# Four steps to a partition: rows of x and of the output in pieces of 4 KB, and the output product reading rwkv at every fourth step

## The reference

```python
xx = jnp.pad(x, ((0, 0), (1, 0), (0, 0)))[:, :-1]
xk = x * time_mix_k + xx * (1.0 - time_mix_k)        # xv, xr likewise
k = jnp.einsum('btc,dc->btd', xk, Wk)                # v, and sr = sigmoid(...), likewise
w = -jnp.exp(time_decay)
rwkv = sr * _wkv(w, time_first, k, v)                # a recurrence over the steps
attn = jnp.einsum('btc,dc->btd', rwkv, Wo)
x = _layernorm(x + attn, axis=-1)
gate = x @ wg.T; up = x @ wu.T                       # weights are int32 values times 1/127
x = _layernorm(x + (silu(gate) * up) @ wd.T, axis=-1)
```

## Time and profile before

| | us |
|---|---|
| median of 3 runs | 290.96 |
| lowest, highest | 290.49, 291.65 |
| the profiled execution | 292.65 |
| its span, from first to last instruction | 290.8 |

### The profile page before, as it was taken

The page is one execution under the profiler, slowest core; times in us unless marked ns, Lnnn a source line. Parts: engine busy times, 40 slices in busy tenths (PEclk is TensorE's granted clock), DMA queues, the critical chain, the costliest instruction groups (busy, mean ns, idle before and its releaser), DMA issues.

```text
span 290.8 us, 4281 instructions
## 1 busy us (share of the span) xinstructions
PE 274.8 (95%) x1258; PEld 199.7 (69%) x1258; DVE 260.5 (90%) x451; ACT 215.1 (74%) x388; POOL 192.0 (66%) x155
## 2 busy tenths in 40 slices
PE   7999988889999999999999999999999999999990
PEld 5745555646695689657885679558974789778890
DVE  4995599899999998999999999999899999889763
ACT  3486798389667988689966986698858882799472
POOL 3637699979968875986868775986566580334043
PEclk9999999999999999999999999999999999999996
DMA  7900600220102202030204011210201020102003
GB/s 239 371 4 0 220 1 0 72 72 3 36 0 76 72 1 72 18 129 0 72 5 133 11 37 35 72 36 0 72 22 51 1 74 0 36 2 73 0 3 113
DMA packets 13541, 16.26 MB, mean 56 GB/s; under 512 B 720, under 2 KB 11216, under 8 KB 13520
## 3 DMA queue, kind: packets, MB, share of 16 engines
q1 hardware_dynamic: 12832, 15.48, 16.3%
q10 hardware_dynamic: 688, 0.53, 0.6%
HBM read 11.81 MB, written 4.19 MB: 55 GB/s over the span
## 4 chain that ended last, share of the span: by engine, by line
PE 74%; DVE 12%; ACT 9%; issue 2%; DMA 1%; SPq 0%; DVEq 0%; ACTq 0%
PE bank_b L1153 12%; PE bank_a L1153 12%; PE bank_a L1176 11%; PE bank_b L1109 9%; PE bank_a L1072 7%; PE bank_d L1072 7%; PE bank_c L1072 7%; PE bank_b L1130 2%; DMA wkT<-wk 1%; DVE rwkv L786 1%; DVE state L746 1%; ACT L605 1%; PE bank_d L1099 1%; ACT wts L491 1%; PE bank_d L1088 1%
## 5 line engine op out<-in xcount | busy, mean ns | idle before, releaser
L403 POOL TENSOR_TENSOR hlo<-hid,hhi 128x512 fp32r<-128x512 f32 (+1 forms) x36 | 53.3, 1484 | 31.6 <-ACT hhi L583 31.5
L376 POOL TENSOR_SCALAR wts<-gap,par 128x512 f32<-128x512 f32 (+1 forms) x18 | 35.9, 1994 | 25.4 <-DVE gap L714 24.6
L499 ACT ACTIVATE mix<-dx,par 128x512 f32<-128x512 f32 x48 | 31.4, 712 | 19.0 <-POOL dx L356 19.0
L1176 PE MATMUL bank_a<-wd_r,hhi 128*128 128x256 f32 x180 | 44.2, 287 | 1.0 <-POOL hlo L403 0.9
L1176 PE MATMUL bank_a<-wd_r,hlo 128*128 128x256 f32 x180 | 42.8, 279 | 0.0
L362 POOL TENSOR_TENSOR mix<-mix,xt 128x512 f32<-128x512 f32 (+1 forms) x36 | 40.7, 1163 | 0.3 <-ACT mix L499 0.3
L1176 PEld LDWEIGHTS bank_a<-wd_r,hhi 128*128 128x128 f32 x180 | 33.8, 188 | 3.5 <-issue 2.6
L583 ACT ACTIVATE hhi<-hid 128x512 fp32r<-128x512 f32 (+1 forms) x54 | 31.0, 576 | 4.7 <-DVE hid L862 4.7
L491 ACT ACTIVATE wts<-wts 128x512 f32<-128x512 f32 (+1 forms) x54 | 27.9, 577 | 8.4 <-DVE wts L723 8.2
L862 DVE TENSOR_TENSOR hid<-bank_b,act 128x512 f32<-128x512 f32 (+1 forms) x48 | 30.8, 643 | 3.6 <-issue 1.1
L1176 PEld LDWEIGHTS bank_a<-wd_r,hlo 128*128 128x128 f32 x180 | 33.8, 188 | 0.3 <-issue 0.2
(11 more groups left out here) (127 smaller groups left out, 600.0 us busy)
## 6 DMA issues: line engine op xcount, KB each, us to landing
xrow<-x SPq DMA_DIRECT2D x7, 512.0 KB, 3.8
xt<-xT SPq DMA_DIRECT2D x6, 513.0 KB, 3.6
out<-y_buf SPq DMA_DIRECT2D x6, 512.0 KB, 2.9
wg_i<-wg SPq DMA_DIRECT2D x1, 768.0 KB, 8.4
wu_i<-wu SPq DMA_DIRECT2D x1, 768.0 KB, 9.8
wd_i<-wd SPq DMA_DIRECT2D x1, 768.0 KB, 11.5
out<-y_buf SPq DMA_DIRECT2D x3, 256.0 KB, 2.2
xt<-xT SPq DMA_DIRECT2D x2, 257.0 KB, 2.9
```

Source lines behind the costliest of these rows:

```text
L376: nc.gpsimd.tensor_scalar(wts[:, OUT, h, 0:n], gap[:, h, 0:n], par[:, FIRST, h:h + 1], CAP, ALU.add, ALU.min).then_inc(out_arg_ready, 1)
L403: nc.gpsimd.tensor_tensor(hlo[:, m, 0:n], hid[:, m % NH, 0:n], hhi[:, m, 0:n].bitcast(f32), ALU.subtract).then_inc(hlo_ready, 1)
L499: nc.scalar.activation(mix[:, s, i, h, 0:n], dx[:, h, 0:n], ACT.Copy, scale=par[:, MIX + i, h:h + 1]).then_inc(dx_scaled, 1)
L1176: mm = nc.tensor.matmul(ffn[:, q, :], hp.bitcast(f32) if full else hp, w[:, m, :], start=(m == 0 and q % 2 == 0 and part is hhi), stop=(m ...
```

## The change

The seven full chunks lay four consecutive steps on one partition: partition p has the steps 4p to 4p + 3 of its chunk, tile q holds the steps 4p + q. In HBM these four rows are one run of 4 KB. The first and the last chunk (256 steps) lay two consecutive steps on a partition. The loads of `xrow` and the stores of `y` name the new rows; for full chunks the view has one run of `n * c` elements (`in_one`). The two part stores of chunk 7 have runs of two rows, 2 KB. Each of the two last stores holds every second row of the last 256.

For `attn` to have the same steps on the same partitions as `xrow`, the output product takes as stationary operand, for tile q, the steps q, q + 4, q + 8 and so on of `rwkv` (every second step in the half chunks). The products behind it don't depend on the order of steps within a chunk, and their code is unchanged; so is the code of DVE, ACT and POOL.

```diff
-    x_v = x.rearrange("(n p) c -> p n c", p=P)
-    out_v = out.rearrange("(n p) c -> p n c", p=P)
+    half = N // 2
+    full_rows = slice(half, half + (NC - 2) * N)
+
+    x_first = x[0:half, :].rearrange("(p n) c -> p n c", p=P)
+    x_full = x[full_rows, :].rearrange("(k p n) c -> p k (n c)", p=P, n=NT)
+    x_last = x[full_rows.stop:, :].rearrange("(p n) c -> p n c", p=P)
+    out_first = out[0:half, :].rearrange("(p n) c -> p n c", p=P)
+    out_full = out[full_rows, :].rearrange("(k p n) c -> p k (n c)", p=P, n=NT)
+    out_last = out[full_rows.stop:, :].rearrange("(p n) c -> p n c", p=P)
...
-            def rows(c):
-                return bass.ds(0 if first(c) else c * NT - NT // 2, steps(c) // P)
+            def in_one(tile):
+                return tile.rearrange("p (o n) c -> p o (n c)", o=1)
...
-                sp.dma_start(xrow[:, 0:steps(c) // P, :],
-                             x_v[:, rows(c), :]).then_inc(xrow_in, 16)
+                if first(c) or last(c):
+                    sp.dma_start(xrow[:, 0:NT // 2, :], x_first if first(c) else x_last).then_inc(xrow_in, 16)
+                else:
+                    sp.dma_start(in_one(xrow[:, :, :]), x_full[:, bass.ds(c - 1, 1), :]).then_inc(xrow_in, 16)
...
-                sp.dma_start(out_v[:, rows(c), :], y[:, 0:steps(c) // P, :]).then_inc(stored, 16)
+                if first(c):
+                    sp.dma_start(out_first, y[:, 0:NT // 2, :]).then_inc(stored, 16)
+                else:
+                    sp.dma_start(out_full[:, bass.ds(c - 1, 1), :], in_one(y)).then_inc(stored, 16)
...
-                sp.dma_start(out_v[:, bass.ds(c * NT - NT // 2, 2), :], y[:, 0:2, :]).then_inc(stored_tail, 16)
+                sp.dma_start(out_full[:, c - 1:c, 0:2 * C], in_one(y[:, 0:2, :])).then_inc(stored_tail, 16)
...
-                sp.dma_start(out_v[:, bass.ds(c * NT - NT // 2 + 2, 2), :], y[:, 2:4, :]).then_inc(stored_tail, 16)
+                sp.dma_start(out_full[:, c - 1:c, 2 * C:], in_one(y[:, 2:4, :])).then_inc(stored_tail, 16)
...
-                sp.dma_start(out_v[:, bass.ds(c * NT - NT // 2 + q, 1), :], y_last[:, q:q + 1, :]).then_inc(stored_tail, 16)
+                sp.dma_start(out_last[:, q:q + 1, :], y_last[:, q:q + 1, :]).then_inc(stored_tail, 16)
...
+                rows = rwkv[:, :, 0:steps(c)].rearrange("p h (t q) -> p h q t", t=P)
                 for q in range(steps(c) // P):
                     for h in range(CH):
-                        mm = nc.tensor.matmul(attn[:, 2 * q if last(c) else q, :], rwkv[:, h, q * P:(q + 1) * P], woT[:, h, :],
+                        mm = nc.tensor.matmul(attn[:, 2 * q if last(c) else q, :], rows[:, h, q, :], woT[:, h, :],
                                               start=(h == 0), stop=(h == CH - 1))
```

## The result

The changed kernel takes 293.81 us in the median of six runs (293.27 to 294.43). The kernel before, run six times in all by then, takes 291.46 us (290.49 to 292.08). The ratio is 1.0085, with a 95% interval of 1.0063 to 1.0108: slower by 0.9%, some 2.4 us. The prediction had 290.8 us and a range up to 293.2, so the time lies above it.

What follows compares the result with a forecast made beforehand. The prediction took PE to bound the steady rounds, with transfers off the chain. Output product 0 + 0.1, loads 0 and stores -0.3 made -0.2 us, from 290.96 to 290.8 us, range 289.4 to 293.2 us.

Steps and rivals of the forecast that it cites:

- Rival (b): Output product L1109: the strided load costs about twice as much; 292.2 us, at the most 294.6; chance 0.11.
- factor "between one and two": Weight loads of L1109: a 16-byte step lengthens the load's 108 to 120 ns by this factor, still within 217 ns.
- the steady distance: Output product L1109: matmuls stay 217 ns apart, 16 in 3.47 us, since they cover the load; put at 0.
- the first loads: First load of each of nine output products, partly uncovered: 0.1 us, bounded by 0 and 1.0 us.
- The loads of `x`: Loads of `x` in 4 KB pieces: at most 1 us shorter each, but nothing waits for them; worth 0.
- The stores: Last stores at the end: fewer outstanding pieces shorten the final held issue; 0.3 us gained, bounds 0 and 1.35.
- The other reading: Final store's issue: held by an engine fetching a 16 KB instruction block (queue q8), not by the outstanding pieces.
- rival (c): Output product L1109: the load becomes its bound beyond 217 ns; 306 us at factor three, 321 at four; chance 0.11.
- Rival (a): End of the kernel: the last store's issue is no longer held, near 0.5 us; 289.7 us in all; chance 0.15.
- Rival (d): DVE and ACT: fewer packets leave engines and memory freer, 1.8 us gained; 289.0 us; chance 0.03.

Runs made afterwards that it cites:

- e8_moving_16_bytes: The kernel before with the moving operand of the projections (f32) and gate and up products (fp32r) read in 16-byte steps; 446.62 us in one run.
- e6_down_step_16_bytes: The kernel before with the down product of the seven full chunks reading its stationary operand at every fourth step, 16 bytes apart; 329.0 us in one run.
- e1_pieces_alone: The changed kernel's new pieces and last store rows, but the output product reads rwkv in order again; 291.11 us against 291.05 for the kernel before, ratio 1.0004.
- e2_read_alone: The kernel before with only the output product's strided read of rwkv, old pieces and rows kept; 293.63 us against 291.05, ratio 1.0080.
- e3_two_steps: Full version of the change with two steps to a partition instead of four, rwkv read 8 bytes apart; 291.59 us against 291.05 for the kernel before, ratio 1.0016.
- e7_down_step_8_bytes: The kernel before with the down product of the seven full chunks reading its stationary operand at every second step, 8 bytes apart; 292.38 us in one run.
- e11_covered_loads: The kernel before with 16-byte steps in the weight loads of projections k, v and r, output product untouched; 292.20 us against 291.49, ratio 1.0016.

## Why the prediction was wrong

**The bound was read right, the price was not.** The steady rounds are bound by PE, and every nanosecond in them is paid. Rival (b) is what happened: the load costs about twice as much, the time was given as 292.2 us with 294.6 as its end, and it had a chance of 0.11. The step that failed is the choice of a factor "between one and two" for the load. It rested on the rate of the moving operand of L1176 (256 columns in 120 ns), read as room on the load's path. That is another operand of another type. At a step of 16 bytes it has no room either: in `e8_moving_16_bytes` a moving fp32r operand goes from 0.46 to 0.90 ns a column, while in `e6_down_step_16_bytes` the load takes 1.84. No row of the trace before bears on a strided load, so the whole width from one to four was open, and nothing favoured its lower half. Rival (b) named the right mechanism, but put 0.5 us on a term that it bounded by 0 and 2.9. The measured factor is 235 / 120 = 1.96 if the contiguous load holds its path for the 120 ns of the down product, and 2.2 with the 108 ns worked out from the single column; the cover ends at 217 ns. Two terms of the sum fell with this step: the steady distance, put at 0, which is 7 products by 15 distances by 18 ns, 1.9 us; and the first loads, put at 0.1 us.

**The sum, redone.** Seven full chunks by 16 loads pay, not 128: in the half chunks the step is 8 bytes and costs nothing (their products take 1.73 and 2.00 us, before 1.73 and 1.99), which the prediction passed over. Seven by (3.86 - 3.47) = 0.39 us are 2.7 us. One of the seven is given back whole: in chunk 1 the product takes 4.12 us, but the path from its start to that of the next product is 31.93 us after and 31.91 before. Chain rows of before, then of after, show how:

```profile
53.38 3.73 PE bank_b L1109 x16
...
59.16 0.92 DVE pmax L707
...
60.24 0.73 DVE shift L842
60.97 1.19 DVE pmax L707
...
85.29 3.45 PE bank_b L1109 x16
```

```profile
52.18 4.12 PE bank_b L1122 x16
58.35 0.55 DVE pmax L719
59.43 0.36 DVE shift L854
59.79 1.25 DVE pmax L719
...
84.11 3.83 PE bank_b L1122 x16
```

DVE comes 0.4 us later and finds its next short step at half its length (0.36 us for 0.73). The pair without and with the strided read shows the same, 0.73 us in `e1_pieces_alone` and 0.34 in `e2_read_alone`; why the step is shorter stays open. In chunk 7 a part is given back too: from the start of its product to that of the last one it is 25.58 us before and 25.82 after, 0.24 us for 0.39, since in the kernel before the chain runs over DVE there. The sum is then 2.7 - 0.4 - 0.15 = 2.2 us, the 2.2 us counted between the first and the last product; by the medians it is 2.35 us, and for the read alone 2.3 us (ratio 1.0080 of 291.05 us). In the tail, four matmuls of the gate and up products of chunk 8 take 0.47 us where they took 0.45. That goes with neither half of the change: it is 0.47 in `e3_two_steps` and 0.45 in `e7_down_step_8_bytes` too.

**First loads: mis-sized.** They were put at 0.1 us, bounded by 1.0. The surplus is 0.13 us in a product (0.36 us to the second matmul for 0.23), and in chunk 1, where PE had waited for `rwkv`, it is the same (0.45 for 0.32). Seven of them are 0.9 us, a third of the 2.7. `e11_covered_loads` has one by itself, 0.12 us.

**The loads of `x`: right.** Nothing waits for them, and `e1_pieces_alone` gives 1.0004. The packets fell to 7909 and not to 8300: the half chunks' loads and the first store, said to keep 1 KB pieces, have 2 KB ones as well, 384 packets fewer.

**The stores: wrong in mechanism, and small.** The 0.3 us were put on fewer outstanding pieces. The rows that follow are the issues of the two last stores, of the changed kernel, of `e2_read_alone` (old pieces) and of `e1_pieces_alone` (new pieces), against the 2.38 us of the earlier trace rows:

```profile
287.36 0.92 SPq L323 DMA_DIRECT2D out<-mix  x2
```

```profile
287.55 0.95 SPq L311 DMA_DIRECT2D out<-mix  x2
```

```profile
284.47 2.87 SPq L323 DMA_DIRECT2D out<-mix  x2
```

The hold doesn't follow the pieces. The two issues take 2.2 to 2.9 us in five of the nine profiles with the old pieces and in three of the four with those of 4 KB, and 0.9 to 1.0 us in the rest. The other reading, the block of instructions (queue q8, one packet of 16 KB), fits better but not wholly. Such a packet is fetched in all fourteen profiles. It starts 0.4 to 0.8 us after the first of the two issues in the eight that are held, and 1.2 us or more after it in five of the six that aren't; in the sixth, `e7_down_step_8_bytes`, it starts at 0.6 to 0.8 us and the two issues take 0.97 us all the same. So the cause stays open. It hardly matters besides: from the end of DVE's last operation to the end of the span it is 4.1 us before and 3.9 us after.

**The mechanism of rival (c)**, the load as the bound of the output product, was right in kind: it decides where a load holds its path for longer than 217 ns, and 235 ns is just beyond. Its sizes, for factors three and four, were not. Rival (a) had its sign in the profile after, where the last issue isn't held (0.92 us for the two), and yet not its gain: 0.2 us came of it and not 1.35. Rival (d) falls with the ratio of 1.0004 in `e1_pieces_alone`.

## What to carry to other kernels

A stride in the stationary operand is a change to TensorE's own work: compare the distance of the matmuls that cover it with the time for which the load holds its path, and count 16-byte pieces for that, here 1.84 ns each, where 128 f32 columns in order stood 120 ns apart. Count the first load of a product apart from the others: its cover is what runs ahead of the product, here 0.13 us short. A step of 8 bytes, or matmuls 430 ns apart, made the stride all but free here, and a step of 12 bytes cost 0.07 us a product; larger DMA pieces were worth nothing where no engine waited for a transfer. Where the price of an operation is in no row of the trace, its own experiment with no cover (here the down product at a distance of 120 ns) comes before any estimate.

## What the runs showed of the hardware

- A weight load of 128 columns is listed with 190, 196, 252, 329 and 337 ns at steps of 4, 8, 12, 16 and 32 bytes; without cover it sets a distance of 120, 123 and 235 ns at 4, 8 and 16 bytes, and beside matmuls that stand 216 ns apart one of 234 ns at 16 bytes and 239 at 32. The Trainium skill, "SBUF — State Buffer", section "Door 1: The DMA port swizzle", asks for two hits on each 16-byte line for full bandwidth. The loads agree: two elements to a line at 8 bytes cost next to nothing, one at 16 bytes doubles the time.
- By the same rule of the Trainium skill a moving fp32r operand at 8 bytes, with two hits on each line, should keep its full rate. The trace doesn't agree: 453 ns for 512 columns where it took 233, and 461 ns at 16 bytes. A moving f32 operand goes from 430 to 450 and 900 ns.
- DVE's f32 multiplication of 1024 elements goes from 1.22 to 2.03 us when it reads both inputs at 16 bytes, and to 2.00 us when it writes at 512 bytes instead.
